# The rows of C in a selective scan: copied by DMA over the partitions in place of TensorE and ScalarE

## The reference, cut to what matters

```python
def step(h, inp):                       # one token t of the 1024 tokens of an image
    u_t, d_t, B_t, C_t = inp
    dA = jnp.exp(d_t[..., None] * As)
    h = h * dA + (d_t * u_t)[..., None] * B_t[:, :, None, :]
    y = jnp.einsum('bkcn,bkn->bkc', h, C_t)
    return (h, y)
```

## Time and profile before

| | |
|---|---|
| runs | 2240.36, 2245.09, 2246.75 us; median 2245.09 us |
| profiled execution, span from first to last instruction | 2244.7 us (its time beyond the span is not listed apart) |
| busy in the span: PE, DVE, ACT, POOL | 1984.1 us (88%), 1575.2 us (70%), 1144.9 us (51%), 1297.0 us (58%) |
| first and last scan start (L1705) | 255.7 us, 1406.8 us |
| first and last readout start (L604) | 260.6 us, 1409.2 us |
| DMA | 229.13 MB, mean 102 GB/s; 65 to 105 GB/s in nearly every slice of the scan |
| granted TensorE clock | 0.968 of full speed in the mean |

### The profile page before, as it was taken

One profiled execution on the slowest core, in us unless ns is written; L12 is line 12 of the kernel. 1 busy time (PEld: TensorE's weight loads), 2 busy tenths in 40 slices (PEclk: granted clock), 3 DMA queues, 4 the chain that ended last, 5 costly groups with the idle time before them and its releaser, 6 DMA issues.

```text
span 2244.7 us, 20167 instructions
## 1 busy us (share of the span) xinstructions
PE 1984.1 (88%) x5826; PEld 919.6 (41%) x5830; DVE 1575.2 (70%) x1505; ACT 1144.9 (51%) x1258; POOL 1297.0 (58%) x464
## 2 busy tenths in 40 slices
PE   7988588888888888888888888989995999999997
PEld 3332133333333333333333333456653555555554
DVE  6978999999999999999999999774553000000000
ACT  4788666666776676776767666211213112122111
POOL 0110499999999999999999999401233011111110
PEclk9987599999999999999999999999997999999999
DMA  6448622233222233222232220611226233333300
GB/s 193 151 175 280 212 75 75 70 98 79 84 66 65 75 100 91 65 75 75 61 105 67 77 73 19 229 42 57 85 85 223 85 119 124 123 119 126 126 24 7
DMA packets 82402, 229.13 MB, mean 102 GB/s; under 512 B 14031, under 2 KB 40257, under 8 KB 80816
## 3 DMA queue, kind: packets, MB, share of 16 engines
q1 hardware_dynamic: 76208, 211.54, 29.6%
q0 software_dynamic: 6144, 16.98, 2.1%
HBM read 166.39 MB, written 64.03 MB: 103 GB/s over the span
## 4 chain that ended last, share of the span: by engine, by line
PE 46%; DVE 23%; issue 17%; POOL 8%; ACT 3%; DMA 1%; DVEq 0%; SPq 0%; ACTq 0%; POOLq 0%
DVE arena L1705 15%; PE ps L1489 11%; PE ps L1502 11%; PE ps L1229 6%; POOL arena L604 4%; POOL arena L587 4%; PE ps L1439 3%; PE ps L1213 2%; PE ps L1110 2%; DVE ps L1688 1%; PE ps L1226 1%; PE ps L1139 1%; PE ps L1390 1%; PE ps L1428 1%; DVE arena L1572 1%
## 5 line engine op out<-in xcount | busy, mean ns | idle before, releaser
L604 POOL TENSOR_TENSOR arena<-arena 128x2048 f32<-128x2048 f32 x192 | 868.3, 4533 | 16.6 <-DVE arena L1705 15.7
L1229 PE MATMUL ps<-arena 128*128 128x512 f32 x1536 | 727.7, 596 | 27.7 <-POOL arena L604 27.6
L1705 DVE TENSOR_TENSOR_SCAN arena<-arena,ps 128x1024 f32<-128x1024 f32 x264 | 587.5, 2266 | 0.0
L880 ACT ACTIVATE arena<-ps 128x1024 f32<-128x1024 f32 x384 | 390.7, 1017 | 248.0 <-PE ps L1213 246.1
L1213 PE MATMUL ps<-arena 96*128 (+1 forms) x1296 | 366.7, 384 | 129.3 <-DVE arena L1705 112.7
L1229 PEld LDWEIGHTS ps<-arena 128*128 128x128 f32 x1536 | 288.4, 190 | 287.7 <-issue 194.0
L587 POOL TENSOR_TENSOR arena<-arena 128x1024 f32<-128x1024 f32 x120 | 283.1, 2359 | 103.5 <-DMA arena<-b_rows 103.5
L2066 DVE TENSOR_TENSOR arena<-ps,arena 128x384 f32<-128x384 f32 x32 | 17.8, 557 | 450.4 <-PE ps L1502 450.4
L1688 DVE TENSOR_TENSOR ps<-ps,arena 128x1024 f32<-128x1024 f32 x264 | 309.1, 1216 | 12.6 <-PE ps L1213 12.6
L873 ACT ACTIVATE arena<-arena 128x1024 f32<-128x1024 f32 x264 | 300.8, 1139 | 8.9 <-DVE arena L1705 8.3
L1213 PEld LDWEIGHTS ps<-arena 96*128 96x128 bf16 x1296 | 112.9, 98 | 461.3 <-DVE arena L1705 215.7
(11 more groups left out here) (225 smaller groups left out, 1611.9 us busy)
## 6 DMA issues: line engine op xcount, KB each, us to landing
arena<-b_rows SPq DMA_DIRECT2D x240, 256.0 KB, 4.2
arena<-in_w SPq DMA_DIRECT2D x16, 2304.0 KB, 13.3
delta<-arena SPq DMA_DIRECT2D x24, 512.0 KB, 2.9
delta_x<-arena SPq DMA_DIRECT2D x24, 512.0 KB, 3.1
arena<-delta SPq DMA_DIRECT2D x24, 512.0 KB, 3.6
arena<-delta_x SPq DMA_DIRECT2D x24, 512.0 KB, 4.6
slot_in<-arena SPq DMA_DIRECT2D x8, 772.0 KB, 8.1
arena<-slot_in SPq DMA_DIRECT2D x8, 772.0 KB, 18.0
```

The lines of the kernel that those rows point to most:

```text
L604: nc.gpsimd.tensor_tensor(hst[:, h:h + 2], hst[:, h:h + 2], c_sb[:, c:c + 2], ALU.mult).then_inc(p2_ok, 2)
L880: nc.scalar.activation(c_sb[:, u % RING], C_PS, ACT.Copy).then_inc(c_free, 1)
L1229: mm = pe.matmul(Y_PS[:, h * 512:(h + 1) * 512], ident, hst[:, u % HRING, h * 512:(h + 1) * 512], start=False, stop=(u == UN - 1))
L1705: nc.vector.tensor_tensor_scan(h, f, x, 0.0, ALU.mult, ALU.add).then_inc(sc_ok, 1)
```

## The change

`spread` of C on PE, its copy on ACT, the bank pair C_PS and the semaphores between them are gone. In their place `c_rows` on SP brings the rows of C of two units by two DMAs (one for each image, 64 partitions by 2048 numbers, 512 KB each) from DRAM straight into two slots of `c_sb`. The readout on POOL waits for these two DMAs in place of the copies. So that C stands in DRAM in fp32, `b_full` now takes all 128 rows before the scan, and `store_parts` stores 64 rows of it where it stored 32 and half as many bf16 parts.

```diff
+C_AT = 20
...
+            def c_rows(U):
+
+                q, u = divmod(U, UN)
+                dr, n = divmod(u, N)
+                slot = U % RING
+                if U >= RING:
+                    sp.wait_ge(p2_ok, U + 2)
+                for im in range(2):
+                    at = SR + im * N + n
+                    sp.dma_start(c_sb[H2 * im:H2 * im + H2, slot:slot + 2].rearrange("p u s -> p (u s)"),
+                                 row_dram[q // J, dr, at:at + 2].rearrange("n s -> (n s)").partition_broadcast(H2)).then_inc(c_ld[slot // 2], 16)
...
+            for k in range(2):
+                sp.wait_ge(bc_st[k], K * NP // 2 * PLACED)
+            c_rows(0)
+            c_rows(2)
             for u in POOL_UNITS[ROWS_EARLY:XRING]:
                 b_row(0, u)
...
+            c_rows(4)
+            c_rows(6)
...
                 if U % UN in POOL_UNITS and U > POOL_UNITS[XRING - 1]:
                     b_row(U // UN, U % UN)
+                if U % 2 == 0 and U >= C_AT:
+                    c_rows(U - C_AT + RING)
...
                     pool.wait_ge(sc_ok, U + 4)
-                    pool.wait_ge(c_free, U + 3)
                     h, c = u % HRING, u % RING
+                    pool.wait_ge(c_ld[c // 2], q * (32 * UN // RING) + 32 * (u // RING + 1))
                     nc.gpsimd.tensor_tensor(hst[:, h:h + 2], hst[:, h:h + 2], c_sb[:, c:c + 2], ALU.mult).then_inc(p2_ok, 2)
...
-                nc.scalar.activation(b_full[0:H2 + SR], slot[0:H2 + SR], ACT.Copy).then_inc(hi_ok, 1)
+                nc.scalar.activation(b_full, slot, ACT.Copy).then_inc(hi_ok, 1)
...
-                    act.wait_ge(c_ok, U + 1)
-
-                    act.wait_ge(p2_ok, U + 1)
-                    if first and C_OVER_MAKE <= u < RING:
-                        act.wait_ge(dm_st[u - C_OVER_MAKE], NP * HALVES // MADE * 32)
-                    nc.scalar.activation(c_sb[:, u % RING], C_PS, ACT.Copy).then_inc(c_free, 1)
...
                     if at == 1:
                         add_trailing_y(q, u - 1, first)
-                    pe.wait_ge(c_free, U + 1)
-                    spread(q, u, 1, C_PS).then_inc(c_ok, 1)
                     if at:
                         add_trailing_y(q, u, first)
```

More of the change, by code:

```diff
@@ L193, in hybrid_block_kernel @@
         rb = Region(arena, XY, BCD)
-        bc = rb.take(2, 2, 2, S, dtype=BF16)
+        bc = rb.take(2, 2, S, dtype=BF16)
         dlt, dux = rb.take(2, S), rb.take(2, S)
@@ L296, in hybrid_block_kernel @@
         B_PS = [pair_of_banks(0), pair_of_banks(2)]
-        C_PS, Y_PS = pair_of_banks(4), pair_of_banks(6)
+        Y_PS = pair_of_banks(6)
         OP_PAIR, OP_BACK, OP_SEEN = (2, 4, 6, 4), (8, 4, 8, 4), 8
@@ L322, in hybrid_block_kernel @@
         xf_ok, tap0_ok, xc_ok, caff_far = sem("xn_far_ready"), sem("first_tap"), sem("x_convolved"), sem("far_affine")
-        cpe_ok, slot_out = sem("conv_filled"), sem("conv_out_of_slot")
+        cpe_ok = sem("conv_filled")
         ab_ok, u_ok, w_ok, pd_ok = sem("abs_ready"), sem("u_ready"), sem("w_ready"), sem("delta_uncorrected")
@@ L333, in hybrid_block_kernel @@
         b_ld = [sem(f"b_row{i}") for i in range(XRING)]
+        c_ld = [sem(f"c_rows{i}") for i in range(RING // 2)]
         dt_ok, d_ok, du_ok = sem("dt_filled"), sem("delta_ready"), sem("delta_x_ready")
-        b_ok, c_ok, c_free, dec_ok = (sem(n) for n in ("b_spread", "c_spread", "c_copied", "decay_ready"))
+        b_ok, dec_ok = (sem(n) for n in ("b_spread", "decay_ready"))
         p1_ok, sc_ok, p2_ok, ya_ok, yev_ok = (sem(n) for n in ("input_ready", "scanned", "readout_ready", "y_added", "y_evacuated"))
@@ L369, in hybrid_block_kernel @@
         LD_C = 16 * (len(CONSTS) + 1 + K)
-        PLACED = 16 * 2 * PART
+        PLACED = 16 * PART
         block = ctx.enter_context(nc.Block())
@@ L410, in store_parts @@
                     for dr in range(2):
-                        for m in range(2):
-                            lo = H2 * dr + m * SR
-                            sp.dma_start(bc_dram[x, part * SR:part * SR + SR, dr, m], parts[lo:lo + SR, o, part]).then_inc(bc_st[o], 16)
+                        lo = H2 * dr
+                        sp.dma_start(bc_dram[x, part * SR:part * SR + SR, dr], parts[lo:lo + SR, o, part]).then_inc(bc_st[o], 16)
                 sp.wait_ge(hi_ok, 2 * x + 1)
                 for dr in range(2):
-                    sp.dma_start(b_dram[x, dr], b_full[H2 * dr:H2 * dr + SR]).then_inc(rows_st[o], 16)
+                    sp.dma_start(row_dram[x, dr], b_full[H2 * dr:H2 * dr + 2 * SR]).then_inc(rows_st[o], 16)
             def store_delta(p, i):
@@ L491, in _ @@
                     b_row(U // UN, U % UN)
+                if U % 2 == 0 and U >= C_AT:
+                    c_rows(U - C_AT + RING)
                 if U % (J * UN) == N and J * UN <= U < 3 * J * UN:
-                    sp.wait_ge(c_ok, U - N)
+                    sp.wait_ge(b_ok, U // UN * VEC_UNITS)
                     load_bc(U // (J * UN) + 1)
+            for U in range(NQ * UN - C_AT + RING, NQ * UN, 2):
+                c_rows(U)
             def load_z(c):
@@ L1206, in _, with spread @@
                         x_proj("xd", *DT_ROWS_AT[p, s])
-            def spread(q, u, m, dst):
+            def spread(q, u, dst):
                 dr, n = divmod(u, N)
@@ L1213, in spread @@
                     mm = pe.matmul(dst[:, h * 512:(h + 1) * 512], sel_lhs[0:BR, n],
-                                   bc[0:BR, q % OJ // J, dr, m, h * 512:(h + 1) * 512], start=True, stop=True)
+                                   bc[0:BR, q % OJ // J, dr, h * 512:(h + 1) * 512], start=True, stop=True)
                 return mm
@@ L1248, in tile_steps @@
                         pe.wait_ge(sc_ok, U + 1)
-                        spread(q, u, 0, B_PS[u % 2]).then_inc(b_ok, 1)
+                        spread(q, u, B_PS[u % 2]).then_inc(b_ok, 1)
                     if at == 1:
                         add_trailing_y(q, u - 1, first)
-                    pe.wait_ge(c_free, U + 1)
-                    spread(q, u, 1, C_PS).then_inc(c_ok, 1)
                     if at:
```

10 lines of the change are left out of this document (3 added, 7 removed).

## The result

The changed kernel takes 2367.97 us (median of four runs, 2358.65 to 2370.24), against 2243.83 for the kernel before on the same chip: a ratio of 1.055, 95% interval 1.0527 to 1.0572. That is 124 us slower.

What follows compares the result with a forecast made beforehand. VectorE and GpSimd (POOL) were taken as full, so relieving PE and ACT gains nothing while DMA becomes a third full engine. 2244.7 + 55.5 (11 changes of tile) + 10 (first tile) - 1 = 2309 us; range 2252 to 2390.

Steps and rivals of the forecast that it cites:

- the first rival: Whole tile: DMA is the bound at 1.2 us for 256 KB, 106.4 us a tile, 2365; 0.22 together with the clock.
- the sum had 65: Whole kernel: 2244.7 + 55.5 for changes of tile + 10 for the first tile - 1 = 2309 us.
- T0: Change of tile: end of the last scan of the tile before, which the deltas wait for; first C forecast at T0 + 13.0.
- the price of 1.1 us: DMA: each 256 KB over 64 partitions takes 1.1 us, so 4.4 us for a pair's 1 MB of C.
- DMA's 98.0 us fit into it: Whole tile: DMA's load of 92.4 + 5.6 = 98.0 us fits into the forecast tile of 101.4 us.
- the tile of 101.4: Steady tile: POOL's own 95.2 us plus 6.25 us of waits gives 101.4 us, where it lasted 96.4.
- the 4.15 and 2.1 of the forecast: Change of tile: POOL waits 4.15 us for the first pair's C rows and another 2.1 us for the second's.
- The lead stays 8.85 us: Change of tile: POOL's first readout starts 8.85 us after the last scan's end, since POOL's lateness delays both alike.
- this decides it: SP's queue at the change of tile: C behind deltas and unit 11's B makes POOL wait, +5.05 us a tile.
- The first tile: Start of the scan: C of units 8 and 9 lands late, near 295, costing +10 us.
- The clock rival: PE at its lower clock level: up to 33 us more, 2342; 0.22 together with DMA as the bound.
- C as fast as the deltas: Rival for C transfers: 0.70 us for 256 KB, 24 us lost, 2269; chance 0.14.

## Why the prediction was right and where it failed

The edits, put on one after another, lead back to the kernel before:

| Kernel | us | step | the step's edit alone on the changed kernel |
|---|---|---|---|
| as changed | 2368.0 | | |
| C over 128 partitions | 2278.5 | -89.5 | -89.5 |
| and early in the order | 2255.3 | -23.2 | -5.6 |
| and work for PE | 2245.6 | -9.8 | +1.8 |
| the kernel before | 2244.5 | | |

**Direction and place: right.** The measured 2368 lies above the forecast's own 2285 to 2335, in the stretch of the first rival: the loss is 124 us where the sum had 65. POOL and DVE bound the kernel, the relief of PE and ACT gave nothing, and the loss is POOL's wait for rows of C. With rate, order and clock mended the time is that of the kernel before and no better (2245.6), though ACT keeps its relief. The landings at the change of tile came out too, T0 + 12.8 and 19.7 where 13.0 and 19.6 were forecast, but in part by luck: unit 11's B landed at T0 + 8.0 and not 8.6, and a pair of C then took 4.74 us and not 4.4.

**The steps that failed in size: the price of 1.1 us, and "DMA's 98.0 us fit into it".** B's price was right for B (its pairs land 2.23 us apart). A quarter megabyte of C costs 1.19, the upper bound of 1.2 that I had from the earlier trace rows and did not take. With it the load is 64 x 1.19 + 20 x 1.12 + 5.6 = 104 us, above the tile of 101.4 in which 98.0 was to fit. So DMA is the bound all through the tile. That is the first rival, with its sign (readouts that wait for C all through the tile) and its place. Its number, 106.4 us for a tile and 2365 in all against 105.84 and 2368, is nearer than its terms: it priced B at 1.2 too and took all twelve tiles alike, where the first lost 16.1 us and the last 1.8. I gave it 0.22, since B's rows never ran that slowly; but those are 256 KB each, in pieces of 4 KB and in short bursts. A margin of 3% between two loads rested on a price known only to 9%.

The price is not all of it. With C in pieces of 4 KB it was the forecast's 1.10, and the time was 2340 and not 2309: of the 59 us that the forecast lacked, 28 came back with the price and 31 did not. On the mean of ten tiles POOL waits there 2.9 and 2.1 us for the first two pairs, near the 4.15 and 2.1 of the forecast; but also 2.7 us at the middle of the tile and 1.2 near its end, where I counted nothing. A load of deltas, sent only after a half's last scan, lands 3.8 us behind the landing before it, where its second transfer takes 1.3: some 2.5 us are lost, twice a tile. 98.0 and 5 us more do not fit into 101.4. This part is read from the trace; no run has pieces of 4 KB and the early order together.

**"The lead stays 8.85 us" failed with it.** The argument held T0 and POOL together over POOL's last work of a tile without idle time. But POOL waited inside that work, 0.29 us for C and 2.40 us for a scan, and was ready at 801.66 - 1.22 = 800.44, T0 + 11.6; at the end of the tile shown it waited 2.41 us for C there. So the first wait of this tile was 1.2 us and not 4.15. The sum of the waits in a tile is set by DMA's load over the whole of it, not by its start.

**The order, "this decides it": too early.** It decides only where the rate does not. By itself it gave 5.6 us (within the spread of these runs), behind the mended rate 23. **The first tile** cost 16 us where I had 10. Its start came near: the readout of units 8 and 9, forecast near 295, began at 296.56:

```profile
296.56 4.51 POOL L625 TENSOR_TENSOR arena<-arena 128x2048 f32<-128x2048 f32 x1 [6.26 <-DMA arena<-bc_rows]
```

The rest are waits later in that tile, for which the forecast had nothing.

**The clock rival** gave nothing on the changed kernel (+1.8 us with PE kept busy, at a clock of 0.96) and is real under it, 10 us, where I let it stand for up to 33. **C as fast as the deltas** fell with the price; even over 128 partitions a quarter took some 0.77 us (3.1 us for 1 MB, worked out above) and not 0.70.

## What to carry to other kernels

When work moves from an idle engine to a queue, work out that queue's load over the whole tile at the worst price that the trace has for such transfers, and compare it with the tile before asking about order: if the queue may be full, latencies at one place decide nothing. Losses can lie in layers, and an edit that does nothing alone can be worth 23 us under another; so take causes away one on top of the other, too, before calling one of them false. A transfer of the same bytes over all 128 partitions is the first thing to try where one over 64 fills the DMA engines; here the layout, with one image on each half, doesn't allow it.

## What was not expected of the hardware

- 512 KB to partitions 32 to 95 cost about 1.7 us, to 0 to 63 2.37: same count, same bytes, DMA share 0.58 against 0.69.
- DMA can read 0.99 busy while it moves 229 GB/s, and 0.78 while it moves 244: the busy share tells that pieces are under way, not that the engines run at their best.
- The granted clock at a change of tile, 0.50 for 3.4 us while the last `add_y` run, was enough to turn a wait of 0.42 us into 1.68 (1.4 to 1.7 at seven of eleven changes); two matmuls a unit that nothing reads brought the clock back to 1.00 and returned 10 us.
- C in pieces of 4 KB, changing sides every 256 KB, cost 1.10 us for a quarter megabyte, and in pieces of 8 KB, changing every 512 KB, 1.19. Why is left open; no run took the length of a piece and the change of sides apart.
